# Merged and reordered transfers at the seams, and a top-two choice made in two parts, in a four-block graph and expert kernel

## The chip, the core and the metric

The kernel runs as one program on one core of a Trainium2 chip. The metric is the time of one execution on the device in microseconds (us). The engines are named as the profile names them: PE (TensorE, matmuls; PEld its weight loads), DVE (VectorE), ACT (ScalarE), POOL (GpSimd) and SP (SyncE, which here only issues transfers; SPq is its queue in the trace). Every engine runs its own list of instructions in order and meets the others through semaphores.

## The reference

3,125 tokens of 256 numbers go through four blocks, each added to its input. What this change touches lies behind the first block.

```python
x = x + graph_layers(layernorm(x))                 # 3 layers, mean over in-neighbours
x = x + experts0(layernorm(x) * gamma + beta)      # 8 experts, each token to its best 2, softmax of 2, gelu
h = layernorm(x)
msg = h[src] + relvectors[edge_type]               # 50,000 edges, 16 relation vectors
red = segment_sum(msg, dst)
x = x + gru(red, h)                                # sigmoid gates r and z, tanh candidate
x = x + experts1(layernorm(x))                     # 16 experts, best 2, softmax of 2, relu, then layernorm * gamma + beta
```

## The kernel before

The tokens are padded to 25 tiles of 128 (`NT`). A stage is a block of the program: five lists of instructions, one for each engine, with a barrier behind it, so that a stage starts when the slowest engine of the last one has ended and what it stored has landed. A loop over the tiles (`tile_loop`) writes out its first and last tiles and runs the others as a hardware loop of four tiles a turn. What sets the order on an engine is the order in the code. Nothing is scheduled by a planner.

In time the stages are these. **build_counts** and **run_layers** do the graph block. **route** chooses the two best experts of each token, counts the tiles of each expert and computes where every token goes. In it DVE runs eleven operations over a 128 x (25 x E) array (L1174 to L1187), then counts, then waits (`numbered`) for a table that POOL makes (`number`, L1270), and goes on with the tile counts (L1200). **run_experts** gathers a tile of tokens at a time (POOL, L1371), multiplies it through an expert and scatters the result (POOL, L1382) to `dr.chosen`: row n holds the first choice of token n, row 3200 + n the second. Its loop turns in pairs: with the tile counts of this input, both odd, POOL scatters one tile more than there are (it repeats an old one), and two gathers stand between and around its last scatters. A scatter waits until the one before it has landed.

**relate** has two passes. In the first, SP loads for each tile `x` (L1536) and the two choices (two transfers, L1538) four tiles ahead, stores the sum `x2` (L1549) and the normed rows `hn` of the tile before (L1542), in this order: wait for the sum, three loads, store of `x2`, store of `hn`. DVE mixes the three (L1666, L1673), norms (L1645) and splits the result in two halves with ACT; L1673 waits until the store of two tiles earlier has landed (`stored`), for `out` has two buffers. PE follows with eight matmuls a tile (L1578) as soon as ACT has written the low half. After the last tile ACT and DVE split the 16 relation vectors into the last tile (L1635, L1696, L1637). In the second pass PE sums for the other 17 tiles of rows (L1597), and SP stores them.

**gru** first turns the weights on PE (L1944), then runs over the tiles: PE turns the inputs of the next tile (L1954, `turn`; it waits for all three loads of a tile, `red`, `hn` and `x`), and multiplies (L1966, L1970); DVE and ACT make the gates. SP starts with five transfers of biases, router and shift, and only then loads tiles. Tokens are normed a few tiles later (DVE, L2124, in the order of `NORMED_AT`), turned by PE (L1979), copied by ACT (L2031, `copy_token`) and scored by PE (L1985). At the end ACT copies the tokens 15, 16 and 17 before the tanh of tile 24 (L2047), DVE finishes tile 24, norms tokens 18 and 19, waits for the deviation of the last five (ACT, L2024, behind the copies of 18 and 19), norms them and waits for all scores. SP stores the normed tokens, POOL adds the shift to each.

**combine** loads the two choices of a tile (two transfers, L1742), mixes them on PE (L1777, L1778), norms on DVE (L1831, L1808, L1811, L1838, L1820) and stores (L1757). `out` has two buffers here too.

## Time and profile before

| what | us |
| --- | --- |
| median of three runs | 1700.25 |
| the three runs | 1699.76 to 1701.4 |
| the profiled execution | 1701.26 |
| its span in the profile | 1698.8 |

The profile covers one execution. A row of the stretches gives the busy time of each engine in a stretch, in the order PE, PEld, DVE, ACT, POOL, and then the granted clock of PE (1.00 is 2.4 GHz, 0.50 is 1.2 GHz), the mean busy share of the 16 DMA engines and the rate. In a row of the timeline the first number is the start, the second the length of one instruction (or of a run of like ones, with their count), and the bracket is the idle time just before it and what ended it; "issue" there means that the profile shows nothing that was waited for. Matmul ends are modelled.

### The profile page before, as it was taken

Reading aid. Unit: us, or ns where it says so; the run is one execution under the profiler, and the core shown is the slowest. Engines: PE = TensorE matmul, PEld = TensorE weight load, DVE = VectorE, ACT = ScalarE, POOL = GpSimd, SP = SyncE. Lnnn points to the kernel's source line nnn. Section 1 sums busy time; section 2 is a strip of 40 time slices with the busy share of each in tenths; the row PEclk is TensorE's granted clock in tenths of the full one; section 3 lists DMA queues with packets and bytes.
Section 4 is the critical chain, followed back from the end, with each engine's and each line's share of the span. In section 5 each row is a group of like instructions: output and inputs, shape, how many; then the busy total and the mean of one; then the engine's idle time right before and its main releaser. Section 6 shows DMA issues by size and latency. Waiting matters only on the chain. (4 is left out here: it accounts for less than half of the span.)

```text
span 1698.8 us, 33464 instructions
## 1 busy us (share of the span) xinstructions
PE 1499.6 (88%) x8652; PEld 1054.0 (62%) x8652; DVE 846.4 (50%) x2425; ACT 486.1 (29%) x1258; POOL 338.3 (20%) x393
## 2 busy tenths in 40 slices
PE   3796799999999999985999957898999849999977
PEld 3685654458444855544999942344566639999864
DVE  6897753233333467775222238511588762232227
ACT  2565320013000311112454433100223314444434
POOL 3000220003000310003555530000001224555430
PEclk9555899999999999996999979999999859999989
DMA  4000331124112332222233347401222244332435
GB/s 127 0 0 1 94 96 49 49 78 133 53 47 59 124 97 83 84 75 100 93 98 118 118 126 238 137 25 53 76 65 65 93 166 158 121 119 94 143 99 181
DMA packets 134635, 158.57 MB, mean 93 GB/s; under 512 B 16929, under 2 KB 119698, under 8 KB 134258
## 3 DMA queue, kind: packets, MB, share of 16 engines
q1 hardware_dynamic: 122642, 125.59, 23.7%
q0 software_dynamic: 11840, 32.12, 6.2%
q8 instruction: 24, 0.39, 0.1%
q14 instruction: 33, 0.27, 0.1%
q10 hardware_dynamic: 96, 0.20, 0.0%
HBM read 103.12 MB, written 57.93 MB: 95 GB/s over the span
## 5 line engine op out<-in xcount | busy, mean ns | idle before, releaser
L898 PE MATMUL layer_ps<-parts,counts 128*128 128x512 f16 x1875 | 409.1, 379 | 1.2 <-issue 0.6
L898 PEld LDWEIGHTS layer_ps<-parts,counts 128*128 (+1 forms) x1875 | 183.3, 98 | 217.8 <-issue 2.8
L1444 ACT ACTIVATE experts_hT<-experts_ps_h,experts_b_col 128x128 f32<-128x128 f32 x456 | 160.9, 368 | 102.3 <-PE experts_ps_h L1419 80.9
L1427 PE MATMUL experts_ps_y<-experts_rows,experts_hT 128*128 128x256 f32 x688 | 163.9, 381 | 0.8 <-ACT experts_hT L1444 0.2
L1382 POOL DMA_INDIRECT chosen<-experts_y,experts_row x116 | 114.6, 988 | 151.4 <-issue 130.0
L1427 PEld LDWEIGHTS experts_ps_y<-experts_rows,experts_hT 128*128 128x128 f32 x688 | 124.2, 190 | 16.1 <-ACT experts_hT L1444 2.5
L799 POOL TENSOR_TENSOR parts<-layer_rest,gru_rows 128x256 f32 (+2 forms) x75 | 54.4, 726 | 392.5 <-DVE layer_rest L774 392.5
L1371 POOL DMA_INDIRECT experts_fetched<-tokens,experts_index x120 | 116.1, 967 | 75.1 <-issue 46.6
L960 DVE COPY layer_total<-layer_ps 128x256 f32<-128x256 f32 x75 | 31.8, 425 | 183.6 <-PE layer_ps L898 180.7
L1419 PEld LDWEIGHTS experts_ps_h<-experts_xT,experts_rows 128*128 128x128 f32 x976 | 120.1, 194 | 4.0 <-DVE experts_xT L1460 0.9
L1419 PE MATMUL experts_ps_h<-experts_xT,experts_rows 128*128 128x128 f32 x976 | 120.6, 277 | 0.5 <-DVE experts_xT L1460 0.5
L730 ACT COPY layer_hT<-layer_ps_t 128x256 f32<-128x256 f32 x75 | 27.7, 369 | 306.3 <-PE layer_ps_t L697 305.6
L1468 DVE COPY experts_xT<-experts_ps_x 128x256 f32<-128x256 f32 x114 | 48.4, 425 | 132.4 <-PE experts_ps_x L1408 126.6
L1419 PEld LDWEIGHTS experts_ps_h<-experts_xT,gru_rows 128*128 128x128 f32 x848 | 104.5, 194 | 4.2 <-DVE experts_xT L1460 0.9
L1419 PE MATMUL experts_ps_h<-experts_xT,gru_rows 128*128 128x128 f32 x848 | 105.1, 278 | 0.7 <-DVE experts_xT L1460 0.5
L538 PE MATMUL ps_counts<-is_place,is_row 128*128 128x125 f16 x636 | 82.5, 295 | 26.0 <-DVE is_node L396 24.9
L598 ACT CAST counts<-ps_counts 128x500 f32 (+1 forms) x159 | 81.3, 584 | 74.4 <-PE ps_counts L543 74.4
L1597 PE MATMUL relate_ps<-parts_rel,counts 128*128 128x512 f16 x425 | 93.5, 383 | 3.8 <-DVE relate_out L1708 3.8
L1966 PE MATMUL gru_ps_g<-gru_wT,gru_xT 128*128 128x512 f32 x200 | 92.3, 605 | 0.1
L538 PEld LDWEIGHTS ps_counts<-is_place,is_row 128*128 128x128 f16 x636 | 68.2, 126 | 29.0 <-issue 25.3
L2146 POOL TENSOR_TENSOR x<-x,gru_shift 128x256 f32<-128x256 f32 x25 | 18.7, 764 | 336.1 <-DVE tokens L2124 336.1
L1448 ACT COPY experts_x<-experts_fetched 128x256 f32 x114 | 46.1, 405 | 136.0 <-POOLq L1367 135.3
(316 smaller groups left out, 2089.1 us busy)
## 6 DMA issues: line engine op xcount, KB each, us to landing
experts_rows<-in_L_ffn_w SPq DMA_DIRECT2D x32, 512.0 KB, 5.1
gru_rows<-x SPq DMA_DIRECT2D x75, 128.0 KB, 2.2
own<-layer_own SPq DMA_DIRECT2D x75, 128.0 KB, 1.7
layer_own_in<-own SPq DMA_DIRECT2D x75, 128.0 KB, 2.1
h<-layer_out SPq DMA_DIRECT2D x50, 128.0 KB, 1.7
gru_rows<-h SPq DMA_DIRECT2D x50, 128.0 KB, 2.1
gru_rows<-chosen SPq DMA_DIRECT2D x50, 128.0 KB, 2.4
combine_y<-chosen SPq DMA_DIRECT2D x50, 128.0 KB, 2.4
```

Of the source, the lines that this page charges most:

```text
L538: nc.tensor.matmul(bank[:, j * PLACES:(j + 1) * PLACES], is_row[b][:, a, :, j], is_place[b][:, a, :, j], start=j == 0, stop=False, skip_gr ...
L598: nc.scalar.copy(cst.counts[:, :, bass.ds((it * BANKS + a) * SUB * WIN, SUB * WIN)].rearrange("p s (j n) -> p s j n", j=SUB), ps[b * BANKS ...
L799: nc.gpsimd.tensor_tensor(parts[live, bass.ds(t, 1), D:2 * D].rearrange("p a d -> p (a d)"), rest[b][live, :], cst.lo_scale[live, :], ALU. ...
L898: last = nc.tensor.matmul(ps[b][:], cst.counts[:, s, bass.ds(t * P, P)], parts[:, s, :], start=s == 0, stop=s == NT - 1)
L1371: pool.indirect_dma_start(fetched[:, b, :], None, dr.tokens, bass.IndirectOffsetOnAxis(ap=index[:, b:b + 1], axis=0)).then_inc(fetch_done[ ...
L1382: pool.indirect_dma_start(dr.chosen, bass.IndirectOffsetOnAxis(ap=row[:, b:b + 1], axis=0), y[:, b, :], None).then_inc(y_stored, 16)
L1419: last = nc.tensor.matmul(ps_h[c][:, 0:P], up[b][:, i, c * P:(c + 1) * P], xT[:, i, :], start=i == 0, stop=i == KD - 1)
L1427: last = nc.tensor.matmul(ps_y[:, 0:D], hT[:, c, :], down[b][:, c, :], start=c == 0, stop=c == KH - 1)
L1444: nc.scalar.activation(hT[:, c, :], ps_h[c][:, 0:P], function, bias=b1_col[:, bass.ds(e * KH + c, 1)]).then_inc(hT_ready, 1)
L1468: nc.vector.tensor_copy(xT[:], ps_x[:]).then_inc(xT_ready, 1)
L1597: last = nc.tensor.matmul(ps[bank][:], cst.counts[:, s, bass.ds(t * P, P)], parts[:, s, :], start=s == 0, stop=s == NT - 1)
L1966: nc.tensor.matmul(ps_g[d][:], xT[d][:, i, c, :], wT[:, i, c, 0:2 * D], start=i == 0 and c == 0, stop=i == 1 and c == KD - 1)
```

## The change

- relate and combine: the two loads of a tile's choices become one transfer of twice the size, through a view of `dr.chosen` with both choices side by side (`dr.both_choices`).
- relate: SP stores `x2` before it loads the tile four ahead. The relation vectors are loaded and split by POOL alone, at the start of the stage; DVE waits for that before the last `remain`.
- run_experts: the loop of POOL ends at the last tile (`plan.last_tile`, one more small DVE operation in route); the last two gathers are gone, and the additional scatter stays.
- gru: SP loads the first two tiles, then the biases, two more tiles, then router and shift. PE waits for the router only at the first score.
- gru: token 18 is normed with 17, in the step of tile 24; ACT copies two tokens (15, 16) before the last tanh where it copied three.
- The second choice of the two best moves from route into the gru stage, behind its last scores, in two parts: tokens of tiles 0 to 19, then 20 to 24 (whose scores now lie in another PSUM bank). The iota of the experts' numbers moves with it. In the first route nothing of this moves.

```diff
 NORMED_AT = {...
-             23: (15, 16), 24: (17,)}
+             23: (15, 16), 24: (17, 18)}
...
+def choose_two(nc, dve, choice, logit, E, part, numbered):
+    n = part.stop - part.start
+    wide = lambda a: a[:, part].unsqueeze(2).to_broadcast([P, n, E])
+    scores, key, expert_no, least = logit[:, part], choice.key[:, part], choice.expert_no[:, part], choice.least[:, part]
+    for c in range(2):
+        top, chosen = choice.top[c][:, part], choice.chosen[:, c, part]
+        nc.vector.tensor_reduce(top, scores, AX.X, ALU.max)
+        dve.drain()
+        nc.vector.tensor_tensor(key, scores, wide(choice.top[c]), ALU.is_equal)
+        dve.drain()
+        if c == 0:
+            dve.wait_ge(numbered, 1)
+        nc.vector.scalar_tensor_tensor(key, key, -100.0, expert_no, ALU.mult, ALU.add)
...
 # route, DVE
+                if logit is not None:
+                    choose_two(nc, dve, choice, logit, E, slice(0, NT), experts_numbered)
...
+                nc.vector.tensor_scalar(plan.last_tile[:], ends[0:1, E - 1:E], -1.0, None, ALU.add)
...
 # run_experts, POOL
-                with pool.Fori(2, pairs) as k:
+                with pool.Fori(2, last + 1) as k:
                     for b in range(2):
                         fetch(k, b)
                         store(k - 1, b)
-                pool.wait_ge(y_stored, pairs * 32 - 32)
                 for b in range(2):
-                    pool.wait_ge(fetch_done[b], pairs * 16 + 16)
+                    pool.wait_ge(fetch_done[b], last * 16 + 32)
+                    pool.sem_inc(fetch_ready, 1)
+                    pool.wait_ge(y_stored, last * 32 + b * 16)
+                    pool.sem_inc(y_free, 1)
+                    pool.wait_ge(row_ready, last * 2 + (b + 1))
+                    pool.wait_ge(y_ready, last * 2 + (b + 2))
+                    store_one(b)
+                pool.wait_ge(y_stored, last * 32 + 32)
...
 # relate, SP
                     sp.dma_start(x[b], dr.x1[rows(t), :]).then_inc(got[b], 16)
-                    for c in range(2):
-                        sp.dma_start(y[b][c], dr.chosen[bass.ds(c * NP + t * P, P), :]).then_inc(got[b], 16)
+                    sp.dma_start(y[b], dr.both_choices[rows(t)]).then_inc(got[b], 16)
...
                     sp.wait_ge(taken, t + 1)
+                    sp.dma_start(dr.x2[rows(t), :], out[b % 2][:]).then_inc(stored[b % 2], 16)
                     if not past(t + B):
                         load(t + B, b)
-                    sp.dma_start(dr.x2[rows(t), :], out[b % 2][:]).then_inc(stored[b % 2], 16)
...
 # relate, POOL
+                pool.dma_start(vectors[rels, :], ins["L1_gnn_relvectors"]).then_inc(v_loaded, 16)
+                nc.gpsimd.memset(parts[REL_ROW:P, NT - 1, :], 0.0)
+                pool.drain()
+                pool.wait_ge(v_loaded, 16)
+                nc.gpsimd.tensor_copy(parts[rels, NT - 1, 0:D], vectors[rels, :])
+                pool.drain()
+                nc.gpsimd.tensor_tensor(vectors[rels, :], vectors[rels, :], parts[rels, NT - 1, 0:D], ALU.subtract)
+                pool.drain()
+                nc.gpsimd.tensor_scalar(parts[rels, NT - 1, D:2 * D], vectors[rels, :], LO_SCALE, None,
+                                        ALU.mult).then_inc(rels_ready, 1)
...
 # combine, SP
-                    for c in range(2):
-                        sp.dma_start(y[b][c][:], dr.chosen[bass.ds(c * NP + t * P, P), :]).then_inc(got[b], 16)
+                    sp.dma_start(y[b][:], dr.both_choices[rows(t)]).then_inc(got[b], 16)
...
 # gru, ACT
-                        for u in range(TAIL, TAIL + 3):
+                        for u in range(TAIL, TAIL + 2):
                             copy_token(u, u)
...
 # gru, DVE
-                dve.wait_ge(scored, NT)
-                nc.vector.tensor_tensor(logit[:], ps_l[:], s_bias[:].unsqueeze(1).to_broadcast([P, NT, E]), ALU.add)
+                for part, scores in zip((slice(0, PART_B), slice(PART_B, NT)), scores_of):
+                    dve.wait_ge(scored, part.stop)
+                    nc.vector.tensor_tensor(logit[:, part], scores, s_bias[:].unsqueeze(1).to_broadcast(
+                        [P, part.stop - part.start, E]), ALU.add)
+                    dve.drain()
+                    choose_two(nc, dve, choice, logit, E, part, experts_numbered)
...
+    dr.both_choices = dr.chosen[0:2 * NP, :].rearrange("(c n) d -> n c d", c=2)
```

SP in the hardware loop of relate's first pass, one tile, before (`gru_rows<-x` and `gru_rows<-chosen` are the loads, `x<-relate_out` the store of `x2`):

```order
L1536 DMA gru_rows<-x 128x256
L1538 DMA gru_rows<-chosen 128x256
L1538 ISA
L1538 DMA gru_rows<-chosen 128x256
L1549 ISA
L1549 DMA x<-relate_out 128x256
L1542 DMA hn<-relate_hn 128x256
L1546 REGISTER_ALU
```

and with the change:

```order
L1569 DMA x<-relate_out 128x256
L1559 ISA
L1559 DMA gru_rows<-x 128x256
L1560 DMA gru_rows<-chosen 128x2x256
L1564 DMA hn<-relate_hn 128x256
L1568 REGISTER_ALU
```

One of five transfers is gone, with the instruction between the two loads, and the store of `x2` stands first.

SP at the start of the gru stage, before:

```order
L1916 DMA gru_bias<-in_L_gnn_b_ih 128x768
L1916 DMA gru_bias<-in_L_gnn_b_hh 128x768
L1926 DMA gru_router<-in_L_ffn_gate_w 128x2x16
L1927 DMA gru_router_bias<-in_L_ffn_gate_b 128x16
L1928 DMA gru_shift<-in_L_ffn_beta 128x256
L1922 DMA gru_x_0<-red 128x256
L1923 DMA gru_x_1<-hn 128x256
L1924 DMA gru_before<-x 128x256
```

and with the change:

```order
L1945 DMA gru_x_0<-red 128x256
L1946 DMA gru_x_1<-hn 128x256
L1947 DMA gru_before<-x 128x256
L1945 DMA gru_x_0<-red 128x256
L1946 DMA gru_x_1<-hn 128x256
L1947 DMA gru_before<-x 128x256
L1950 DMA gru_bias<-in_L_gnn_b_ih 128x768
L1950 DMA gru_bias<-in_L_gnn_b_hh 128x768
```

The three loads of tile 0 had five transfers ahead of them and have none; router, its bias and the shift follow behind the fourth tile.

DVE at the end of the gru stage, before (a branch is the change of the stage):

```order
L2124 TENSOR_SCALAR tokens<-x,x_stats,gru_inv 128x256 x5
L2139 TENSOR_TENSOR logit<-gru_ps_l,gru_router_bias 128x400
L1911 UNCONDITIONAL_BRANCH
L1169 UNCONDITIONAL_BRANCH
L1174 TENSOR_REDUCE route_top<-logit 128x25
L1176 TENSOR_TENSOR route_key<-logit,route_top 128x400
```

and with the change, the end of the second part and what follows it:

```order
L1104 TENSOR_REDUCE choice_top<-logit 128x5
L1106 TENSOR_TENSOR choice_key<-logit,choice_top 128x80
L1110 SCALAR_TENSOR_TENSOR choice_key<-choice_key,choice_expert_no 128x80
L1112 TENSOR_REDUCE choice_least<-choice_key 128x5
L1114 TENSOR_TENSOR choice_chosen<-choice_key,choice_least 128x80
L1932 UNCONDITIONAL_BRANCH
L1205 UNCONDITIONAL_BRANCH
L1209 TENSOR_TENSOR route_either<-choice_chosen 128x25x16
L1213 SCALAR_TENSOR_TENSOR route_upto<-route_first_of,route_either 128x400
```

The eleven operations over 400 columns that stood behind the change of stage now stand before it, as eleven over 320 columns and eleven over 80, each with an addition of the bias ahead.

## Rows read from the trace of the kernel before

**Rows 1.** Stages: start:end, length, busy us (count) by engine; clock, DMA share, GB/s.

```profile
1004.40:1077.30 72.90, 45.09 (x186) 18.41 (x187) 56.18 (x175) 26.57 (x76) 0.52 (x1) 0.90 0.74 225
1077.30:1344.40 267.10, 255.08 (x1050) 144.63 (x1048) 140.70 (x387) 51.57 (x103) 12.70 (x17) 0.97 0.22 67
```

**Rows 2.** SP queue in time, relate's loop: start us, length us, engine, line, what.

```profile
1043.30 0.36 SPq L1536 DMA_DIRECT2D gru_rows<-x  x1
1043.75 0.91 SPq L1538 DMA_DIRECT2D gru_rows<-chosen  x2
...
1046.04 0.35 SPq L1536 DMA_DIRECT2D gru_rows<-x  x1
```

**Rows 3.** Groups on DVE, relate's first pass: count, busy us, mean ns, idle before.

```profile
L1673 DVE SCALAR_TENSOR_TENSOR relate_out<-gru_rows,mix_weight,relate_mixed 128x256 f32<-128x256 f32 x25 | 12.1, 484 | 6.6 <-DMA x<-relate_out 5.9
```

**Rows 4.** DVE in time, relate's first pass, starts of single tiles.

```profile
1007.77 0.48 DVE L1666 SCALAR_TENSOR_TENSOR relate_mixed<-gru_rows,mix_weight 128x256 f32<-128x256 f32 x1 [10.58 <-DMA gru_rows<-chosen]
...
1030.89 0.48 DVE L1666 SCALAR_TENSOR_TENSOR relate_mixed<-gru_rows,mix_weight 128x256 f32<-128x256 f32 x1 [0.48 <-issue]
...
1041.07 0.48 DVE L1666 SCALAR_TENSOR_TENSOR relate_mixed<-gru_rows,mix_weight 128x256 f32<-128x256 f32 x1 [0.43 <-issue]
...
1070.32 0.45 DVE L1666 SCALAR_TENSOR_TENSOR relate_mixed<-gru_rows,mix_weight 128x256 f32<-128x256 f32 x1
...
1072.54 0.45 DVE L1666 SCALAR_TENSOR_TENSOR relate_mixed<-gru_rows,mix_weight 128x256 f32<-128x256 f32 x1
```

**Rows 5.** Page, part 6: transfers, count, KB each, median us from issue to landing.

```profile
experts_rows<-in_L_ffn_w SPq DMA_DIRECT2D x32, 512.0 KB, 5.1
...
combine_y<-chosen SPq DMA_DIRECT2D x50, 128.0 KB, 2.4
```

**Rows 6.** SP and PE in time, start of the gru stage.

```profile
1184.37 0.43 SPq L1924 DMA_DIRECT2D gru_before<-x  x1
...
1191.04 2.19 PE L1954 MATMUL gru_ps_t<-ident,gru_x 128*128 128x128 f32 x8 [4.57 <-DMA gru_before<-x]
1193.03 5.67 PE L1966 MATMUL gru_ps_g<-gru_wT,gru_xT 128*128 128x512 f32 x8
...
1200.70 3.60 PE L1966 MATMUL gru_ps_g<-gru_wT,gru_xT 128*128 128x512 f32 x8
```

**Rows 7.** Stretches at the start of the gru stage, columns as in group 1.

```profile
1187.00:1191.00 4.00, 0.00 (x0) 0.00 (x0) 0.54 (x1) 0.00 (x0) 0.00 (x0) 0.92 0.86 296
1191.00:1197.00 6.00, 5.94 (x13) 3.31 (x14) 0.00 (x0) 1.17 (x2) 0.00 (x0) 0.50 0.25 84
```

**Rows 8.** DVE and ACT in time, end of the gru stage.

```profile
1347.52 0.42 DVE L2104 TENSOR_TENSOR gru_cand<-gru_cand,gru_hidden 128x256 f32<-128x256 f32 x1
...
1355.56 2.94 DVE L2124 TENSOR_SCALAR tokens<-x,x_stats,gru_inv 128x256 f32<-128x256 f32 x5
...
1349.86 0.42 ACT L2047 ACTIVATE gru_new<-gru_cand 128x256 f32<-128x256 f32 x1
...
1354.73 0.37 ACT L2031 COPY gru_scoreT<-gru_ps_t 128x256 f32<-128x256 f32 x1 [0.80 <-PE gru_ps_t L1979]
```

**Rows 9.** The second choice: one tile's instructions (min/median/max ns); then POOL and DVE in time.

```profile
L1184 DVE TENSOR_TENSOR route_chosen<-route_key,route_least x4: 368/472/576, 768.8 to 1370.6; 128x200 f32<-128x200 f32 x2, 128x400 f32<-128x400 f32 x2
...
1363.89 0.59 POOL L1270 IOTA route_expert_no<- 128x400 f32 x1 [4.13 <-POOLq L1911]
...
1366.16 4.81 POOL L1270 IOTA route_number<- 128x3200 f16 x1
...
1374.30 0.17 DVE L1200 TENSOR_SCALAR route_tiles_i<-route_ps_sum 128x16 int32<-128x16 f32 x1 [0.84 <-PE route_ps_sum L1156]
```

**Rows 10.** The combine stage: a DVE group; then one line's instructions, first and last start.

```profile
L1820 DVE SCALAR_TENSOR_TENSOR combine_out<-combine_normal,combine_small,x 128x256 f32<-128x256 f32 x25 | 12.1, 484 | 3.0 <-DMA blocks_out<-combine_out 1.3 <-issue 0.7
...
L1831 DVE BATCH_NORM_STATS2 combine_small<-combine_ps x25: 423/426/433, 1649.0 to 1690.7; 128x6 f32<-128x256 f32 x25
```

**Rows 11.** POOL in time, the last store of the first expert stage.

```profile
1001.49 0.99 POOL L1382 DMA_INDIRECT chosen<-experts_y,experts_row  x1 [1.19 <-issue]
```

More of the change, by code:

```diff
@@ L1079, in tile_ends, with __init__, number_experts, route @@
     return ends
-def route(nc, cst, dr, tag, E, logit, plan, expert_weights, old):
+class Choice:
+    def __init__(self, stack, nc, tag, E):
+        sb = lambda n, s: stack.enter_context(nc.sbuf_tensor(tag + n, s, F32))
+        self.expert_no, self.key = sb("expert_no", [P, NT, E]), sb("key", [P, NT, E])
+        self.chosen = sb("chosen", [P, 2, NT, E])
+        self.top = [sb(f"top{c}", [P, NT]) for c in range(2)]
+        self.least = sb("least", [P, NT])
+def number_experts(nc, choice, E):
+    return nc.gpsimd.iota(choice.expert_no[:], [[0, NT], [1, E]], base=0, channel_multiplier=0,
+                          allow_small_or_imprecise_dtypes=True)
+def choose_two(nc, dve, choice, logit, E, part, numbered):
[12 more added lines that the diff above has]
+        dve.drain()
+        nc.vector.tensor_reduce(least, key, AX.X, ALU.min)
+        dve.drain()
+        nc.vector.tensor_tensor(chosen, key, wide(choice.least), ALU.is_equal)
+        dve.drain()
+        if c == 0:
+            nc.vector.scalar_tensor_tensor(scores, chosen, -3e38, scores, ALU.mult, ALU.add)
+            dve.drain()
+def route(nc, cst, dr, tag, E, plan, expert_weights, old, choice, logit=None):
     with ExitStack() as ctx:
@@ L1271, in _ @@
                                                                          allow_small_or_imprecise_dtypes=True)
-                iota(expert_no[:], [[0, NT], [1, E]], 0)
+                if logit is not None:
+                    number_experts(nc, choice, E).then_inc(experts_numbered, 1)
                 nc.gpsimd.memset(ones[:], 1.0)
@@ L1372, in fetch, with store @@
                         ap=index[:, b:b + 1], axis=0)).then_inc(fetch_done[b], 16)
-                def store(k, b):
-                    first = isinstance(k, int) and k == 0 and b == 0
-                    if not first:
+                def store(k, b, free_one=True):
+                    if free_one:
                         pool.wait_ge(y_stored, k * 32 + b * 16)
@@ L1388, in _ @@
                     fetch(1, b)
-                    store(0, b)
-                pairs = nc.s_assert_within((total + 1) // 2 + 1, 3, most // 2 + 2,
-                                           skip_runtime_bounds_check_because="an expert has a tile")
-                with pool.Fori(2, pairs) as k:
+                    store(0, b, free_one=b > 0)
+                last = nc.s_assert_within(last_tile // 2, (E - 1) // 2, most // 2,
+                                          skip_runtime_bounds_check_because="an expert has a tile")
+                with pool.Fori(2, last + 1) as k:
                     for b in range(2):
@@ L1504, in relate @@
         B = 4
-        y = [[w_rows[:, c, b, :] for c in range(2)] for b in range(B)]
+        y = [w_rows[:, 0:2, b, :] for b in range(B)]
         x = [w_rows[:, b // 2, B + b % 2, :] for b in range(B)]
@@ L1630, in _ @@
                 low(NT - 1, NT - 1)
-                act.drain()
-                act.wait_ge(cleared, 1)
-                act.wait_ge(v_loaded, 16)
-                nc.scalar.copy(parts[rels, NT - 1, 0:D], vectors[rels, :]).then_inc(v_hi_ready, 1)
-                act.wait_ge(v_rest_ready, 1)
-                nc.scalar.activation(parts[rels, NT - 1, D:2 * D], rest[0][rels, :], ACT.Copy,
-                                     scale=LO_SCALE).then_inc(rels_ready, 1)
             @block.vector
@@ L1855, in load_gru_rows, with gru @@
         sp.dma_start(w_rows[:, i], ins[n].rearrange("(g p) d -> p g d", p=P)).then_inc(cst.gru_rows_loaded, 16)
-def gru(nc, ins, cst, dr, w_rows, sums, states, source, result, stats, E, router, router_bias, beta, tokens, logit):
+def gru(nc, ins, cst, dr, w_rows, sums, states, source, result, stats, E, router, router_bias, beta, tokens, logit, choice):
     G = 3 * D
@@ L1996, in _ @@
                 turn(0, 1)
-                pe.wait_ge(r_loaded, 32)
                 def step_and_score(k, b):
@@ L2060, in _ @@
                 nc.scalar.preload_act_table(ACT.Sqrt)
-                for u in range(TAIL + 3, NT):
+                for u in range(TAIL + 2, NT):
                     if u == PART_B:
```

93 lines of the change are left out of this document (41 added, 52 removed).

## The prediction

> **What bounds the kernel now.** I read the stages first, then in each stage the change touches the wait that ends last. In the first pass of relate no engine is full: in 72.9 us PE is busy for 45.1, DVE for 56.2, and the DMA engines at 0.74 [rows 1]. SP is what is full. It gives a turn of one tile per 2.74 us (1043.30 to 1046.04), and its five transfers have next to no gap between them; the two loads of the choices alone take 0.91 us [rows 2]. What DVE sees of it is that the store of `x2`, which stands behind three loads, lands late: L1673 waits 5.9 us for it [rows 3]. From the end of that pass to tile 24 of gru PE is busy for 255.1 of 267.1 us [rows 1], so a us won ahead of it or at its seam is kept. At the start of gru PE waits 4.57 us for the last load of tile 0 [rows 6]. At the end of gru and in route a chain through DVE, ACT and POOL decides, with one tile or one wait at a time.
>
> The sum is made against the profiled execution: span 1698.8, device time 1701.26, which is 1.0 above the median of the three runs. I take that 1.0 off at the end.
>
> **relate, first pass.** One of five transfers goes, 0.45 us of the 0.91 [rows 2], and with its register work about 0.5: SP falls from 2.74 to about 2.25 us a tile. The next limit is DVE. Between 1030.89 and 1041.07 it does four tiles of the hardware loop with no wait for a transfer: 2.545 us a tile, and in the tiles that are written out 2.22 (1070.32 to 1072.54) [rows 4]. So DVE, and no more SP, sets the pace. From the first mix at 1007.77 to the last at 1072.54 are 24 steps in 64.8 us [rows 4]; 16 of them at 2.545 and 8 at 2.22 are 58.5, or 6.3 less. That is the 5.9 us of L1673 and a few tenths of other waits, so the two ways to count agree. The waits go because the store is now issued ahead of the loads, and the prologue of SP has eight transfers before its first store and not sixteen. The first mix itself waits for its second choice, issued one transfer earlier now: 0.3 us. Together **-6.6**. Bounds: -7.5 if the two first steps, which have nothing to split yet, are quicker than 2.22; -3 if only the start is won and the transfers set the pace of the loop (rival 1). The relation vectors go from ACT and DVE to POOL, which idles in this stage; PE is occupied with the tiles before at that time, so I price this at nothing. If that cover were gone it would cost or give a few tenths.
>
> The Trainium skill, "DMA: Bandwidth & Descriptors", section on issuing engines not being separate DMA queues, says that issuing elsewhere saves only the sequencer's time, which is usually small beside the transfer itself. By that rule a merged transfer gives next to nothing, and the sum would lose its loop parts; here the row shows that the issue is not small (0.45 of 2.74 us a tile), so I go by the row.
>
> **gru, start.** The loads of tile 0 stood behind five transfers and landed 6.2 us after the last of them was issued at 1184.37 with its 0.43 (PE starts at 1191.04) [rows 6]; the DMA engines were at 0.86 [rows 7], moving mostly biases. With nothing ahead they are issued in 1.4 us from the start of the stage, and a transfer of this size lands in 2.4 [rows 5], so they are there before PE has turned the weights at 1186.47 (1191.04 less 4.57) [rows 6]. PE then starts after DVE's last copy, about 0.5 later: 4.1 us less idle. In that gap the clock had just risen: 0.92 granted in 1187 to 1191, and 0.50 (1.2 GHz) again in 1191 to 1197 [rows 7], where PE was busy once more. Without the gap PE goes on at 2.4 GHz: the first eight gate products took 5.67 us and at the high level take 3.60 [rows 6], 2.1 less; of the turns before them (2.19 for eight) half is won, but ACT's copy is then waited for, so 0.6; and 0.5 I give back for a late second tile, whose turn stands before the first products. Together **-6.3**. The biases now land behind two tiles, but DVE needs them only at the first product, some 6 us later. Bounds: -7.5 (nothing given back) and -3.5 (the clock stays low for as long as before, rival 2). Later tiles are as early as before, and the router is needed only at the first score.
>
> **gru, end.** DVE has the candidate of tile 24 at 1347.94, but ACT starts its tanh only at 1349.86, behind the copy of token 17 [rows 8]. With that copy behind the tanh, DVE goes on after its norms of 17 and 18, near 1349.2: 1.1 us earlier. And one token fewer has to pass norm, turn and copy before the deviation; one pass is 1.17 us (0.80 idle and 0.37 copy) [rows 8]. So the norms of the last five tokens, at 1355.56 before [rows 8], start 2.2 us earlier, at 1353.4, and end at 1356.3; the last score comes at 1360.8 and not at 1363.0.
>
> **The choice.** One of its operations takes 0.368 us for 200 columns and 0.576 for 400 [rows 9], so 1.04 ns a column on 0.16: 0.493 for 320 and 0.243 for 80, each with 0.075 for the drain. Twelve of the first are 6.8 us, twelve of the second 3.8. The first part starts at 1356.3, while PE still scores, the second ends at 1367.0, and route starts at 1367.3, where it started at 1363.89 [rows 9]. DVE alone would have won: it now needs only the sum and the scan before the tile counts. But POOL starts its table with the stage. `number` ended at 1370.97, 7.08 after the start of route [rows 9]; without the iota that moved out (0.59) it ends about 6.5 us after it, at 1373.8, and DVE waits for it before the tile counts. They start near 1374.0, where they started at 1374.30 [rows 9]. So the 2.2 us of the tail and the eleven operations that leave route are nearly all spent on this wait: **-0.3** for tail and choice together. Queued behind this wait of DVE are the tile counts, then every engine's loop bounds. Bounds: -3.8 if the table is not waited for (rival 3); +1.5 if POOL's additions slow the choice. In the first route I find nothing but the added `last_tile`, about 0.1 us in each route: **+0.2**.
>
> **combine.** SP is late here too. L1820 waits 1.3 us for the store of two tiles before and 0.7 more with nothing visible [rows 10]. Both lie in DVE's chain, which runs at (1690.7 - 1649.0) / 24 = 1.74 us a tile [rows 10] of which its instructions leave little over. With one of three transfers less, SP's turn is shorter than that: **-2.0**, bounds -0.4 (only the earlier first load) and -2.8 (more of the start).
>
> **run_experts.** The last scatter starts at 1001.49 after 1.19 us idle, in which POOL waits for the landing of the one before [rows 11]. The gather that goes stands in front of that idle time, so the landing hides it: -0.1 in each of the two stages, **-0.2**, bounds 0 and -0.6.
>
> Sum: -6.6 -6.3 -0.3 +0.2 -2.0 -0.2 = -15.2. 1701.26 - 15.2 = 1686.1, and 1.0 less for the median: **1685 us**.
>
> **Rivals.**
> 1. *The transfers, not their issue, set the pace.* The bytes are the same, and the DMA engines are at 0.74 over the whole pass [rows 1]; at 2.5 us a tile they would be near 0.85. If they hold at 2.74 us a tile, relate keeps only its start (-3.2) and combine its smaller bound (-0.4): 3.4 and 1.6 less, 1690. For it speaks that landings get longer when it is dense; against it that SP has no gaps to wait in.
> 2. *The clock does not follow.* It may stay at 1.2 GHz after 1187, if the short stops of PE between turns and first products count for it as idle: then 2.8 us of gru's start are not won, 1688. For it: it rose and fell within 4 us here [rows 7].
> 3. *The table is not waited for*, because the iota ends earlier than its row says (spans of POOL are rough): the tile counts then start 3.5 us earlier, 1681.5.
> 4. *The merged load is slow to land.* It reads two places 3.2 MB apart for each row. A load of combine is issued three tiles of 1.74 us ahead of its use. If it took more than 5.2 us to land, each tile would take a third of the landing time; from 6.8 us on that costs 25 x 0.6 = 15 us and the whole gain, and at 8 us combine alone loses 25 x 0.95 = 24, which ends at 1709, slower than before. Against it: 128 KB land in 2.4 us and 512 KB in 5.1 [rows 5], so 256 KB in about 3.3.
> 5. *The change does nothing*, because an engine I take for free (DVE in relate) is the true bound: 1699.
>
> **Chances.** The forecast (1682.5 to 1687.5) 0.55; rival 1 0.14; rival 2 0.12; rival 3 0.11; rival 4 0.03; rival 5 0.02; small effects in nobody's list 0.03. The range takes in the first three rivals with the bounds of the terms: 1678.5 to 1692. About 0.2% (3.4 us) is what a measurement of this kernel can tell from no change: faster than that 0.94, within it 0.03, slower 0.03.
>
> **What would show it.** Right: relate's first pass has DVE at 2.2 to 2.55 us a tile and no wait of L1673's successor for its store; PE's first turn in gru follows the weights within 1 us, and the clock in the 6 us after it is near 1.00; in the second route DVE waits for POOL before the tile counts, which start within 1 us of where they were, counted from the last product of gru; combine is some 2 us shorter. Wrong: a wait of DVE for `gru_rows<-chosen` inside the loops (rivals 1 and 4), low clock behind the weights (2), tile counts without a wait (3).

## The result: 5 us won, a third of the forecast

The changed kernel takes 1694.72 us in the median of 12 runs (1691.35 to 1696.88), the kernel before 1699.78 in 12 runs beside them. The ratio is 0.9968 with an interval of 0.9959 to 0.9976: faster beyond its interval, by 5 us and not by 15, and slower than the 1692 us at which the stated range ends. A second measurement (e4 below) gives 0.9965 [0.9954, 0.9976].

The profiled execution of the changed kernel took 1696.88 us (span 1694.0), 4.4 less than the profiled one of before. Where the stages stand now (start:end, length, busy us and count of PE, PEld, DVE, ACT and POOL, clock, DMA share, GB/s); first relate's first pass, then gru up to PE's first turn and from there to the first candidate:

```profile
1011.40:1077.90 66.50, 45.88 (x185) 18.48 (x186) 56.32 (x175) 25.00 (x75) 1.98 (x3) 0.91 0.80 237
...
1178.30:1187.50 9.20, 5.35 (x24) 4.87 (x25) 3.40 (x8) 3.44 (x7) 0.59 (x1) 0.63 0.47 142
1187.50:1197.20 9.70, 9.46 (x35) 5.62 (x36) 2.81 (x6) 1.70 (x3) 0.00 (x0) 0.99 0.51 138
```

The second row is where PE waited for the loads of tile 0 before, the last row is the stretch that ran at 1.2 GHz for its first 6 us before [rows 7]: the granted clock is now 0.99. PE and SP at the same place, in time:

```profile
1181.55 0.35 SPq L1945 DMA_DIRECT2D gru_x<-red  x1
...
1187.50 1.11 PE L1979 MATMUL gru_ps_t<-ident,gru_x 128*128 128x128 f32 x8 [0.56 <-ACT gru_wT L2044]
1188.85 3.70 PE L1991 MATMUL gru_ps_g<-gru_wT,gru_xT 128*128 128x512 f32 x8 [0.24 <-ACT gru_xT L2048]
```

The 4.57 us of waiting for a transfer [rows 6] are 0.56 for the copy of the weights, and the first eight gate products take 3.70 and not 5.67 us. This part went as forecast.

In relate it didn't. DVE's groups, first mix to last (count, busy us, mean ns, idle before and what ended it); then what landed when (count, KB, median us to landing):

```profile
L1688 DVE SCALAR_TENSOR_TENSOR relate_mixed<-gru_rows,mix_weight 128x256 f32<-128x256 f32 x25 | 11.9, 477 | 13.3 <-DMA gru_rows<-chosen 11.2 <-issue 1.8
L1695 DVE SCALAR_TENSOR_TENSOR relate_out<-gru_rows,mix_weight,relate_mixed 128x256 f32<-128x256 f32 x24 | 11.6, 485 | 0.9
L1667 DVE TENSOR_SCALAR relate_hn<-relate_out,relate_small 128x256 f32<-128x256 f32 x23 | 9.4, 411 | 2.6 <-DMA hn<-relate_hn 2.4
...
gru_rows<-chosen SPq DMA_DIRECT2D x22, 256.0 KB, 3.8
x<-relate_out SPq DMA_DIRECT2D x24, 128.0 KB, 2.7
hn<-relate_hn SPq DMA_DIRECT2D x23, 128.0 KB, 3.6
```

In the kernel before, the same wait and the same landing were these:

```profile
DVE relate_hn L1645 <- DMA hn<-relate_hn: 0.7, 1, 0.7
...
hn<-relate_hn SPq DMA_DIRECT2D x23, 128.0 KB, 2.2
```

The wait for the store of `x2` (5.9 us, [rows 3]) is gone, but L1667 now waits 2.4 us for the store of `hn` of two tiles before. That store stands last in SP's turn, as it did before, but now right behind the merged load. The 11.2 us of the first line are the wait ahead of the first mix (10.4) and one of 0.8 us for the choices of the second tile. In combine the wait for the store grew, where it was meant to go away: the 1.3 us of [rows 10] are 3.6, and PE waits 4.4 us for its loads, where it waited 1.1 (the last line is of before).

```profile
L1837 DVE SCALAR_TENSOR_TENSOR combine_out<-combine_normal,combine_small,x 128x256 f32<-128x256 f32 x23 | 11.2, 485 | 5.3 <-DMA blocks_out<-combine_out 3.6 <-issue 0.7
...
combine_y<-chosen SPq DMA_DIRECT2D x21, 256.0 KB, 3.4
blocks_out<-combine_out SPq DMA_DIRECT2D x22, 128.0 KB, 2.6
...
PE combine_ps L1794 <- DMA combine_y<-chosen: 4.4, 10, 1.1
...
PE combine_ps L1777 <- DMA combine_y<-chosen: 1.1, 3, 0.5
```

At the end of gru and in the second route, DVE and POOL in time:

```profile
1350.23 0.48 DVE L2168 TENSOR_TENSOR logit<-gru_ps_l,gru_router_bias 128x320 f32<-128x320 f32 x1
...
1360.80 0.24 DVE L1114 TENSOR_TENSOR choice_chosen<-choice_key,choice_least 128x80 f32<-128x80 f32 x1
1361.42 0.97 DVE L1209 TENSOR_TENSOR route_either<-choice_chosen 128x400 f32<-128x400 f32 x1 [0.38 <-PEq L1932]
...
1367.74 0.19 DVE L1218 SCALAR_TENSOR_TENSOR route_token_code<-route_token_no 128x25 f16<-128x25 f16 x1 [4.19 <-POOL route_number L1292]
1367.85 0.17 DVE L1221 TENSOR_SCALAR route_tiles_i<-route_ps_sum 128x16 int32<-128x16 f32 x1
...
1362.91 4.80 POOL L1292 IOTA route_number<- 128x3200 f16 x1
```

DVE is done with the scan early and stands 4.19 us for POOL's table, as the prediction said: the tile counts start 27.0 us after the last candidate (1340.89), where it was 26.8 [rows 8, 9].

### The profile page after: what moved, and what is told of

It reads as the page before. It is cut to its first block and busy times, and to the rows that moved or that the text cites. A ratio compares the mean times of both kernels' runs of the same rounds, so it can differ in the third digit from the quotient of the medians.

```text
span 1694.0 us, 33346 instructions
## 1 busy us (share of the span) xinstructions
PE 1499.2 (89%) x8652; PEld 1054.9 (62%) x8652; DVE 848.7 (50%) x2438; ACT 483.3 (29%) x1256; POOL 337.6 (20%) x393
## 5 line engine op out<-in xcount | busy, mean ns | idle before, releaser
L1394 POOL DMA_INDIRECT experts_fetched<-tokens,experts_index x116 | 112.2, 968 | 72.4 <-issue 44.7
L1499 DVE COPY experts_xT<-experts_ps_x 128x256 f32<-128x256 f32 x114 | 48.4, 425 | 126.8 <-PE experts_ps_x L1439 120.6
L718 PE MATMUL layer_ps_n<-gru_rows,layer_hT 128*128 128x256 f32 x300 | 78.2, 384 | 0.0
```

The lines of the kernel that those rows point to most:

```text
L718: last = nc.tensor.matmul(ps[b][:, 0:D], hT[b][:, c, :], weights[:, c, lo:lo + D], start=c == 0, stop=c == KD - 1)
L1394: pool.indirect_dma_start(fetched[:, b, :], None, dr.tokens, bass.IndirectOffsetOnAxis(ap=index[:, b:b + 1], axis=0)).then_inc(fetch_done[ ...
```

## The experiments

All times below are stage lengths read from one profile each, unless a ratio is given. The borders: **relate** from its first mix to its last, **gru start** from the start of the last copy of relate's sums to the first candidate (DVE's product of `gru_cand` and `gru_hidden`), **end** from the last of these to the first tokens that the experts' stage takes up, **combine** from its first statistics to its last.

### Each part undone, on one chip (e1 to e4)

e1 takes relate's SP back to what it was:

```diff
-                    sp.dma_start(y[b], dr.both_choices[rows(t)]).then_inc(got[b], 16)
+                    for c in range(2):
+                        sp.dma_start(y[b][:, c, :], dr.chosen[bass.ds(c * NP + t * P, P), :]).then_inc(got[b], 16)
...
-                    sp.dma_start(dr.x2[rows(t), :], out[b % 2][:]).then_inc(stored[b % 2], 16)
                     if not past(t + B):
                         load(t + B, b)
+                    sp.dma_start(dr.x2[rows(t), :], out[b % 2][:]).then_inc(stored[b % 2], 16)
```

> The changed kernel with relate's SP as it was before: two loads for the choices, and the store of x2 behind the loads. Theory A (the profiled gain of relate is real and small): first to last mix go back from 62.1 to about 64.7 us, and the whole is 2.5 to 3.5 us longer than the changed kernel (0.9984 of the kernel before and not 0.9968). Rival B (relate's gain is the 6.6 us of the prediction, and an unchanged part of the program eats half of it): 6 us or more longer, at the time of the kernel before or above it. Rival C (merging gives nothing at all here, the shorter stage is chance): within 1 us of the changed kernel.

Measured: 0.9979 [0.997, 0.9988], 0.0014 above the changed kernel beside it, that is 2.4 us; relate 64.2 us, 0.2 below the 64.4 to 64.8 of the kernel before, where six profiles with the new SP have 61.0 to 62.4. The two ratios have intervals that overlap, so the timed runs alone don't prove it; the stage does: the small gain is real (theory A), and rival B's 6 us are not there.

e2 is the same loop of two loads in combine's `load`.

> The changed kernel with combine's choices loaded by two transfers again; all else stays merged. Theory A (the merged load of 256 KB stands ahead of the store in the queue, so the store lands later and DVE waits for its out buffer): combine from its first to its last statistics goes back from 43.4 to about 41.7 us, the waits for the store (L1837) from 3.6 to about 1.3 us, and the whole is 1.5 to 2 us shorter than the changed kernel. Rival B (combine's 1.7 us are chance, or come from where its buffers lie): no change beyond 0.5 us. Rival C (the merge does help by the prediction's 2.0 and something else costs 3.7): 2 us longer.

Measured: 0.9969 [0.9959, 0.998], no difference. Combine took 42.1 us, inside the 41.6 to 43.4 of eight profiles with the merged load (mean 42.5). Rival B: the merge is worth nothing that can be seen here, and much of the 1.7 us by which the first profile was longer is scatter. The reason that theory A gave is only half there: with two loads the store lands in 1.9 us, and DVE still waits 2.9 us for it and PE 3.3 us for its loads (1.3 and 1.1 before). Why these waits don't fall back further isn't shown.

e3 puts the loads of the biases and of the router ahead of the tiles again.

> The changed kernel with the biases and the router's loads ahead of the token tiles again at the start of gru. Theory A: the gap of PE ahead of its first turn comes back (4.8 to 8.8 us after the first copy of the weights), the clock falls again behind it, the stage up to its first candidate is 6.5 to 7 us longer, and so is the whole: this one edit then gives more than the change as a whole (5.1 us). Rival B (a late start of gru is caught up later, since loads run ahead): 2 us or less.

Measured: 0.9997 [0.9987, 1.0007], so this edit alone carries nearly the whole gain, 5.4 us beside e4. PE's gap is back, and so is some of the low clock:

```profile
1186.96 2.13 PE L1978 MATMUL gru_ps_t<-ident,gru_x 128*128 128x128 f32 x8 [4.24 <-DMA gru_before<-x]
...
1187.00:1191.00 4.00, 4.00 (x12) 2.57 (x13) 0.00 (x0) 1.17 (x2) 0.00 (x0) 0.62 0.39 125
1191.00:1197.70 6.70, 6.70 (x24) 3.87 (x23) 2.12 (x5) 0.63 (x1) 0.00 (x0) 1.00 0.00 0
```

The low clock lasted about 3 us here (an estimate from the 0.62 granted over the first four), where it lasted 6 in the profile of before [rows 7]: gru's start was 23.6 us, not 25.5.

> The changed kernel as it is, with a new profile. The parts that the change doesn't touch (up to the last logit, the first stage of experts) took 3.0 us longer in its first profile than in that of the kernel before. If they do so by themselves from run to run, they come out another way here, by 1 us or more; if the change lengthens them, 3 us again.

Measured: 0.9965 [0.9954, 0.9976]. Up to the last logit of the first stage it took 765.6 us (767.4 in its first profile, 766.3 before), the first stage of experts 215.5 (217.0 and 215.1), but the second stage of experts 241.4 (237.9 and 238.1). So parts that the change doesn't touch, or hardly, differ by 2 us and more from one execution to the next, and the 3 us by which they were longer in the first profile are not of the change. Some of it may be the chip and not the execution: it isn't known whether the first two profiles are of one chip.

### The kernel before, twice more (e5, e6)

> The kernel before as it is, for a second profile. Five profiles of changed kernels put the changed stages 8 to 9 us below the one profile of before, but the medians differ by 5 to 6 us. Theory A: that one profile of before is long by 2 to 3 us where the clock decides (its stretch at the low clock in gru's start, 12.4 us from PE's first turn to the first candidate, beside 10.7 in the run with the old start), so here the low stretch is shorter, and gru's start is nearer to 23.5 than to 25.5 us. Rival B: the stages of before come out as in its first profile within 0.5 us, and the missing 3 us lie in stages that the change lengthens.

> The kernel before once more, as the run ahead of it: a third profile, to tell the spread of each stage from a shift.

Measured, one execution each: 1702.10 and 1700.98 us. The stages, with those of the changed kernel from all profiles so far and from e7 to e11 below, as far as the stage is unchanged in them:

| us | before, three profiles | changed, as it stands in that stage | forecast | found |
|---|---|---|---|---|
| relate | 64.7, 64.4, 64.8 | 62.1, 61.4, 61.2, 61.0, 62.4, 61.4 | -6.3 | -3.0 |
| gru start | 25.5, 23.6, 24.4 | 17.8 to 18.9, mean 18.3 (9) | -6.3 | -6.2 |
| end | 48.8, 48.4, 48.7 | 48.8 to 49.2, mean 48.9 (8) | -0.3 | +0.3 |
| combine | 41.7, 42.5, 40.4 | 41.6 to 43.4, mean 42.5 (8) | -2.0 | +1.0 |

The start times of the mixes show where relate's 3.0 us lie. The fifth mix begins 8.6 us after the first in e12 below, where DVE waits for no store, 11.4 us after it before (mean of three) and 10.0 in the changed kernel (mean of its first profile and e4). The 16 steps behind it take 2.70 us each before and 2.62 in the changed kernel, and 2.52 and 2.53 in e12 and e11. So the gain of the change is half start and half loop, and neither is all that was there to win.

Theory A of e5 holds in its kind: the one profile on which the gru term was built was long there, by 1.0 us against the mean of three. What before loses at the low clock depends on when it comes back.

### The choice and the table (e7, e8)

e7 leaves `choose_two` and the numbering of experts out of gru and hands `logit1` to the second `route`. e8 moves one instruction of POOL:

```diff
@@ gru, block.gpsimd
                 number_experts(nc, choice, E).then_inc(experts_numbered, 1)
+                nc.gpsimd.iota(choice.number[:], [[1, P], [0, NT]], base=0, channel_multiplier=0,
+                               allow_small_or_imprecise_dtypes=True)
@@ route, block.gpsimd
-                iota(spare_row[:], [[0, 1]], 1, 2 * NP - HALF)
-                iota(number[:], [[1, P], [0, NT]], 0).then_inc(numbered, 1)
+                last = iota(spare_row[:], [[0, 1]], 1, 2 * NP - HALF)
+                if logit is not None:
+                    last = iota(number[:], [[1, P], [0, NT]], 0)
+                last.then_inc(numbered, 1)
```

> The changed kernel with the choice of two and the numbering of the experts in the second route again; the order of the tail and the split logits stay. Theory A (in the changed kernel the second route waits for POOL's table anyway): the time from the last candidate to the first tokens of the experts, 48.9 us, comes out at 48.5 to 50, and the whole within 1 us of the changed kernel. Rival B (moving the choice wins the 4 us that its first part takes, and the tail's order loses them): 52 us or more, the whole 3 us longer.

Measured: 0.9955 [0.994, 0.9971], and the end took 47.1 us, where 48.5 to 50 was expected: neither theory. By this profile the changed kernel would be 1.8 us better off at this place without the move; the ratios (0.9955 beside 0.9965 and 0.9968) lie that way without settling it. POOL's rows of e7 and of the changed kernel tell why:

```profile
1355.23 0.59 POOL L1094 IOTA choice_expert_no<- 128x400 f32 x1 [3.79 <-POOLq L1931]
...
1357.25 4.81 POOL L1292 IOTA route_number<- 128x3200 f16 x1
```

```profile
1361.37 0.11 POOL L1296 MEMSET route_ones_e<- 128x16 f32 x1 [9.79 <-POOLq L1932]
```

With the choice in route the stage begins 14.5 us after the last candidate (1340.7), with the choice in gru 20.5 us after it: POOL stands at the stage's border for 9.79 us while DVE chooses. The table, 4.8 us long and begun some 2 us into the stage, lies beside the choice in one case and behind it in the other. The new order of the tail had won 1.9 us (the stage began 16.4 us after the candidate before [rows 8, 9], and 14.5 in e7), and the move of the choice spent it. In e7 DVE no longer waits for the table: its eleven operations over 400 columns last longer than POOL needs.

> The changed kernel with one more edit: POOL writes the table of place numbers for the second route at the start of gru, where it idles, and not in route. Theory A (DVE waits for this table and for nothing else there): from the sum of the two choices to the tile counts 3.1 us and not 6.4, and the whole 3.3 us shorter than the changed kernel. Rival B (another wait is next, for POOL's other constants or PE's sums): 1 to 2 us shorter. Rival C (the tile counts come earlier, but the experts' first weights or first tokens are not there): nothing.

Measured: 0.9957 [0.9942, 0.9972]; the end 45.5 us, from the sum of the choices to the tile counts 3.2 and not 6.4. Theory A in the profile: without the table only a wait of 0.9 us for PE's sums is left there. The whole gained less than 3.3 us (ratio 0.9957 beside 0.9965 and 0.9968), a difference which these intervals can't settle.

### Order, merge and buffers in relate and combine (e9 to e14)

e9 has the new order with two loads, e10 the merged load ahead of the store of `x2`.

> The changed kernel with two loads for the choices in relate, but the store of x2 still ahead of them: the new order without the merge. Before, the stage takes 64.6 us from first to last mix; changed, 61.6 (mean of six profiles). Theory A (the order does the work, since only the store landed late): 61.5 to 62.5 us, no wait for the store of x2, and SP with no gaps. Rival B (the issue time that the merge saves does it): 64 us or more.

> The changed kernel with the merged load in relate ahead of the store of x2: the merge without the new order. Theory A: the store lands behind 384 KB of loads again, DVE waits for it for 3 us or more, and the stage takes 63 us or more. Rival B (the merge alone is enough, since SP then has time to spare): within 0.7 us of 61.6.

Measured: relate 63.9 us in e9, near what rival B expects, and 62.7 in e10, between the two, with 5.0 us of waiting for the store of `x2` and none for that of `hn`. Neither edit does it alone: the order gives 0.7 of the 3.0 us, the merge 1.9, in one profile each, where six profiles of one version lie 1.4 us apart. In e9 the wait for `x2` is down to 1.0 us in one place, as theory A wanted, but the wait has moved on:

```profile
DVE relate_hn L1668 <- DMA hn<-relate_hn: 4.2, 9, 1.5
...
DVE relate_out L1696 <- DMA x<-relate_out: 1.0, 1, 1.0
```

Two stores of each turn go through two buffers each, and one of them is the last in SP's turn. In e9 it lands in 2.2 us, as before, so it is not the landing that makes it late but its place behind four others in a full queue: in this stage SP waits 4.9 us for DVE in e9 and 14.0 in the changed kernel. e11 puts the stores first in both stages:

```diff
@@ relate, block.sync, step
                     sp.dma_start(dr.x2[rows(t), :], out[b % 2][:]).then_inc(stored[b % 2], 16)
-                    if not past(t + B):
-                        load(t + B, b)
                     if not early(t - 1):
                         store_normed(t - 1, b + 1)
+                    if not past(t + B):
+                        load(t + B, b)
```

> The changed kernel with the stores of hn (relate) and of the result (combine) issued ahead of the loads of the same turn. Theory A (these stores land late because they stand behind the merged load): combine from 42.6 to 41.0 us or less, the store's median landing from 2.6 back to about 2.1, and DVE's wait for it from 3.2 to 4.2 us to below 2; in relate the wait for hn goes from 1.7 to below 1. Rival B (the transfers share the engines whatever their order, so the store is as late as before and the loads now wait for DVE): nothing, or up to 1 us longer in either stage.

Measured (one profile): relate 58.2 us; the forecast of 58.5 had assumed a DVE that waits for no store, and this is that case. L1667 no longer waits, and the landing of `hn` is 2.6 us and not 3.6:

```profile
L1667 DVE TENSOR_SCALAR relate_hn<-relate_out,relate_small 128x256 f32<-128x256 f32 x23 | 9.3, 406 | 0.0
...
hn<-relate_hn SPq DMA_DIRECT2D x23, 128.0 KB, 2.6
```

In combine the same edit gave nothing, as rival B had it, and a little worse: 44.0 us. DVE no longer waits for the store, which lands in 2.2 us and not as late as before, but SP stands ahead of the load until DVE has its result (16.6 us of waiting in all), and PE waits for its loads in 15 places (4.6 us), where it did in 10 (4.4), and DVE 2.2 us longer for PE.

The Trainium skill, "DMA: Bandwidth & Descriptors", section "Queues, rings and completion order", says that on each DMA engine the descriptors are taken in the order of the ring and that the increment which reports a transfer lands only after every earlier write of that engine. The landings agree with it: in relate the same 128 KB store takes 3.6 us behind a load of 256 KB and 2.6 ahead of it, although the stage moves more bytes a us in the second case (263 and not 246 GB/s).

e12 leaves the order as the change has it and gives `hn` in relate and the result in combine four buffers and four semaphores, and adds the table of e8:

```diff
-        hn, rest = pair("hn", [P, D]), pair("rest", [P, D])
+        hn, rest = [sb(f"hn{b}", [P, D]) for b in range(B)], pair("rest", [P, D])
...
-                    if not early(u - 2):
-                        dve.wait_ge(hn_stored[b], use * 16)
+                    if not early(u - B):
+                        dve.wait_ge(hn_stored[h], k * 16)
```

> The changed kernel with the early table of the run before, and four buffers instead of two for hn in relate and for the result in combine, so that DVE doesn't wait for these stores. Theory A (the landing of the stores sets the pace through two buffers): relate 60 us (the pace of DVE without waits), combine 39.5 to 40.5 us, and the end of gru to the experts' first tokens 45.5 us; 4 to 7 us shorter than the changed kernel, 0.993 to 0.994 of the kernel before. Rival B (the loads are then waited for instead): only the 3.4 us of the table are left, 0.9948.

Measured: 0.9915 [0.9901, 0.9929], 1683.54 us: faster than both kernels. Relate 57.8, combine 39.1, end 46.0 us. The transfers of relate land later than in any other version, and it costs nothing, since nobody waits for them (the stage; one of DVE's groups; the landings):

```profile
1007.20:1065.00 57.80, 41.93 (x168) 16.85 (x168) 52.00 (x165) 22.70 (x68) 1.96 (x3) 0.90 0.90 265
...
L1672 DVE TENSOR_SCALAR relate_hn<-relate_out,relate_small 128x256 f32<-128x256 f32 x23 | 9.4, 407 | 0.0
...
gru_rows<-chosen SPq DMA_DIRECT2D x22, 256.0 KB, 4.1
hn<-relate_hn SPq DMA_DIRECT2D x23, 128.0 KB, 3.9
```

And DVE's result in combine, whose idle time of 5.3 us in the changed kernel is down to 1.5, with the store landing in 2.6 us in both:

```profile
L1842 DVE SCALAR_TENSOR_TENSOR combine_out<-combine_normal,combine_small,x 128x256 f32<-128x256 f32 x23 | 11.1, 485 | 1.5
```

e13 and e14 take the merge, and then the order too, out of this version.

> The version with the early table and four buffers, but with two loads for the choices again in relate and combine (the store of x2 still ahead of them). Theory A (with the store buffers out of the way the issue of SP is the next limit, and the merge now pays): relate from 57.8 to 60 us or more, combine from 39.1 to 40.5 or more. Rival B (the buffers alone were the limit, the merge is worth nothing at all): both within 0.7 us.

> As the run ahead of it, and the store of x2 in relate behind the loads, as in the kernel before: four buffers for hn and the results, and nothing else of the relate and combine edits. Theory A: relate near 64 us, since the store of x2 has only two buffers and stands last; combine as in the run ahead. Rival B (hn was the only limit): relate within 1 us of the run ahead.

Measured: relate 62.1 us in e13 and 64.3 in e14, combine 40.5 and 41.3. Theory A for both. With the buffers out of the way the merge is worth 4.1 us in relate (58.0 with it, mean of e12, e15 and e16, beside 62.1) and 1.5 in combine (39.4, mean of the same three, beside 40.9 of e13 and e14); with two buffers it was worth 2.3 in relate (61.6 beside 63.9 of e9) and nothing in combine. What is left in e13 is the store of `x2`, 3.9 us of waiting in DVE.

### The choice once more, and the repeat (e15, e16)

> The version with the early table and four buffers, with the choice of two in the second route again instead of in gru. With the table late this was 1.8 us shorter in the profile (47.1 beside 48.9 us from the last candidate to the experts' first tokens). Theory A (it was shorter only because the table then started 2 us earlier): with the table early there is nothing to hide the choice behind, so it is 1 to 2 us longer than 45.5, at 46.5 to 47.1. Rival B (the choice in two parts costs more than it hides in any case): 45 us or less.

> The version with the early table and four buffers once more, for comparison on the same chip: 0.9915 of the kernel before, relate 57.8, combine 39.1 us, if its first profile was no chance.

Measured: e15 0.9926 [0.9912, 0.994] with an end of 47.2 us; e16 0.9916 [0.9902, 0.993] with an end of 45.9, relate 57.6, combine 40.0. With the table out of the way the choice belongs in gru (1.3 us in the profile, and the ratios lie the same way without settling it), with the table in route it doesn't. The better version repeats on another chip.

## Why the prediction failed, step by step

- **What bounds relate** was right as far as it went: SP's queue was full, the issue of a load was not small, and the transfers themselves were not the pace (in e12 the stage runs at a DMA share of 0.90 and takes 57.8 us). The pace of DVE without waits was right too (2.545 us a tile forecast in the loop, 2.52 and 2.53 found in e12 and e11). **The failed step is "So DVE, and no more SP, sets the pace".** I followed the one store that the profile of before showed late, and not the second one through two buffers. It stood last in SP's turn all the time, hidden behind the wait for `x2` (0.7 us of waiting in one place), and is the next thing to be waited for once that wait is gone: 2.4 us in the changed kernel, 4.2 in e9. The merged load right ahead of it also makes it land later (3.6 us, where it was 2.2). The term of -6.6 measured -3.0; with that store out of the way it is -6.4 (e11) to -7.0 (e16), so it cost some 3.5 us, of which the profile books 2.4 to it. What was missing is one question, asked of each transfer behind the merged one: who waits for it, and through how many buffers.
- The two ways to count that "agreed" in relate were not independent: both took the waits of one line as gone and put none in their place.
- The 0.3 us for an earlier first mix didn't come: 3.31 us from SP's first load to the mix, where it was 3.32. The relation vectors on POOL cost nothing that can be seen.
- **gru, start: right.** -6.3 forecast, -6.2 found against three profiles, the gap and the clock each in its place. e3 gives -5.4 for it by the timed runs.
- **gru, end, and the choice:** the mechanism (a wait for POOL's table eats the gain) was right, and the term of -0.3 was found as +0.3. Of the tail alone I gave 2.2 us; the norms of the last five tokens begin 6.5 us after the last candidate and not 8.0, so it is 1.6, and the wait for the table hid the difference. But "nearly all spent" hid that the tail's 1.9 us would have stayed without the move of the choice. Rival 3's price of 3.5 us for a table that isn't waited for was measured by e8 at 3.3.
- **`last_tile`:** the first route to the experts' stage took 26.4 us in the three profiles of before and 26.7 to 26.9 in all of the changed: 0.4, where I gave it 0.1.
- **combine: no gain, perhaps a loss.** -2.0 forecast, about +1.0 found (42.5 in eight profiles, 41.5 in three of before; each scatters by 1, so the sign isn't certain, and e2 saw no difference). The failed step is that SP's shorter turn would end the wait for the store: the wait grew from 1.3 to 3.6 us. Two result buffers at 1.74 us a tile leave 3.5 us for DVE's write, SP's issue and the landing, and the landing grew from 2.2 to 2.6 us behind the merged load. That last sum is argued, and it isn't the whole cause, since in e2 the store landed in 1.9 us and was waited for all the same; that the buffers were the limit is shown by e12 (39.1) and e13 (40.5), where DVE waits for no store.
- **run_experts:** nothing of 0.2 us can be seen under the scatter of the experts' stages.
- **The rivals:** rival 1 came nearest by its number (1690) and for the wrong reason: transfers did get longer, but they set the pace only through two buffers. It was wrong on the place as well: it left the loop at 2.74 us a tile and kept 3.2 us at the start, and the start gave 1.3 and the loop 1.3. Rival 2 fell (clock 0.99). Rival 5 (nothing changes) fell with e1 and e3. Rival 4's edge stood far off: 256 KB landed in 3.8 us in relate and 3.4 in combine, where 3.3 was estimated and 5.2 was the edge. Its sums were too high besides: at 6.8 us to land a tile takes 2.27 us, 0.53 more than 1.74, which is 13 us and not 15, and at 8 us it is 23.
- The stages found sum to -7.9 (relate -3.0, gru's start -6.2, its loop -0.4, the end +0.3, the first route +0.4, combine +1.0), the two timed measurements to -5.1 and -5.9, with intervals that reach to -7.0 and -7.8. These 2 to 3 us aren't located: the second stage of experts alone (from its first tokens to DVE's last result), which the change hardly touches, took between 237.4 and 241.4 us.

## What to carry to other kernels

When transfers in one queue are merged or reordered, list every transfer that now stands behind the longer one, with its number of buffers and the engine that waits for it; the late one will be the one that the old profile hardly showed. A merge that saves issue time pays in full only where nobody waits for the stores beside it. More buffers did that in both stages here, and the merge was then worth 4.1 us in relate and not 2.3; the stores ahead of the loads did it in relate (58.2 us) but not in combine (44.0), where SP then kept the load waiting for DVE. Work moved ahead of a stage's border delays everything that the other engines start at that border, so move their long constants first.

## What the runs showed of the hardware

- The landing of a 128 KB store depends on what was issued just ahead of it in its queue: in relate 2.2 us behind two loads of 128 KB (e9), 3.6 behind one of 256 KB with the same bytes in the turn (the changed kernel), 3.9 in e12, and 2.6 where it was issued ahead of that load (e11).
- Stages of this kernel that an edit doesn't touch scatter by 1 to 2 us in each profile, and the first stage of experts took 216.6 to 219.6 us on two chips and 214.5 to 216.1 on a third: a term below 2 us needs several profiles or many timed runs.
- After a gap of PE of nearly the same length at the same place (4.57 and 4.24 us) the low clock lasted 6 us in one execution and about 3 in another.
